# Query and key rows of the second attention kept so that a stack row is one 8 KB run in DRAM, read back whole in six transfers

## The reference

```python
Q, K, V = proj(wq, bq), proj(wk, bk), proj(wv, bv)     # [B, 16 heads, 512, 8]
scores = einsum('bhqd,bhkd->bhqk', Q, K) * scale
u = min(L, max(1, int(log(L))))                        # 6
top_u = top_k(scores.max(axis=-1), u)[1]               # the 6 queries with the largest score, per head
q_sel = take_along_axis(Q, top_u)
ctx = softmax(einsum('bhud,bhkd->bhuk', q_sel, K) * scale) @ V
out = zeros.at[top_u].set(ctx) @ wo.T + bo
```

## Time and profile before

| what | value |
|---|---|
| median of three runs | 1387.65 us (1384.28 to 1389.28) |
| the profiled execution: its own time | 1385.65 us |
| its span in the trace | 1383.8 us |
| granted TensorE clock, mean over the span | 0.871 |
| busy: PE, DVE, POOL, ACT | 81%, 75%, 64%, 55% |
| DMA: moved, mean rate | 176.65 MB, 128 GB/s |

### The profile page before, as it was taken

How to read it: one execution, slowest core, us unless ns; L and a number is a source line. 1 busy time by engine, 2 the same in 40 slices (tenths; PEclk the granted TensorE clock), 3 DMA queues, 4 the chain that set the end, 5 groups by cost and what they waited for, 6 DMA issues and landing times.

```text
span 1383.8 us, 27422 instructions
## 1 busy us (share of the span) xinstructions
PE 1121.0 (81%) x7574; PEld 696.9 (50%) x7574; DVE 1040.6 (75%) x4507; ACT 754.2 (55%) x1934; POOL 885.4 (64%) x1342
## 2 busy tenths in 40 slices
PE   3999999897999987888878888888888899999100
PEld 1555555564888972334333333334333379899100
DVE  2899999898475636899989999998988966565211
ACT  2444444342665655777766766766766657556000
POOL 3237776677553503567888888878785555367776
PEclk9999999999899995798898888977868789999655
DMA  6877621102465664444444444444444435577522
GB/s 177 220 192 192 164 70 60 51 31 57 121 187 176 191 174 120 118 112 102 114 105 107 107 112 114 115 120 114 105 105 97 132 89 162 160 217 213 150 76 78
DMA packets 176104, 176.65 MB, mean 128 GB/s; under 512 B 22736, under 2 KB 166224, under 8 KB 175952
## 3 DMA queue, kind: packets, MB, share of 16 engines
q1 hardware_dynamic: 159568, 141.19, 38.4%
q0 software_dynamic: 16384, 33.72, 8.8%
HBM read 83.91 MB, written 90.92 MB: 126 GB/s over the span
## 4 chain that ended last, share of the span: by engine, by line
PE 22%; DVE 21%; POOL 10%; ACT 6%; issue 5%; DMA 3%; SPq 2%; ACTq 0%; POOLq 0%; DVEq 0%
DVE pT L1544 13%; PE pair L2028 5%; PE pair L1951 5%; POOL tok L663 5%; POOL vmyg L663 5%; ACT pT L1059 3%; PE pair L1962 2%; PE pair L1940 1%; PE bank L2069 1%; PE bank L1752 1%; PE bank L2013 1%; DVE xs L1466 1%; SPq L461 1%; PE bank L1758 1%; PE bank L2034 1%
## 5 line engine op out<-in xcount | busy, mean ns | idle before, releaser
L1544 DVE CUSTOM_DVE_ANT_0 pT<-pair,pT 128x256 f32<-128x256 f32 x1024 | 379.6, 414 | 46.8 <-ACT pT L1059 44.3
L1059 ACT ACTIVATE pT<-pair 128x256 f32<-128x256 f32 x1024 | 322.9, 398 | 137.7 <-PE pair L2028 136.9
L1951 PE MATMUL pair<-xeT_sg,unit_w 128*128 128x256 f32 x768 | 183.4, 382 | 0.0
L1269 DVE TENSOR_TENSOR pT<-pair,causal 128x512 f32<-128x512 f32 x256 | 159.4, 679 | 15.5 <-PE pair L1813 15.2
L604 POOL DMA_INDIRECT dispA<-xnf,sli x128 | 128.4, 1003 | 53.9 <-issue 31.6
L2028 PE MATMUL pair<-whose,apart 64*128 64x512 bf16 x512 | 135.3, 454 | 33.7 <-DVE smax L1544 29.7
L604 POOL DMA_INDIRECT dispB<-xnf,sli x128 | 128.5, 1004 | 51.9 <-issue 30.7
L2028 PE MATMUL pair<-xeT_sg,apart 64*128 64x512 bf16 x512 | 132.9, 451 | 31.6 <-DVE smax L1544 30.8
L1436 DVE TENSOR_TENSOR hid<-xeT_sg,pair 128x512 f32<-128x512 f32 x96 | 65.9, 686 | 114.6 <-ACT xeT_sg L969 114.4
L1951 PEld LDWEIGHTS pair<-xeT_sg,unit_w 128*128 128x128 f32 x768 | 139.6, 192 | 15.2
L1962 PE MATMUL pair<-unit_w,hid 128*128 128x128 f32 x768 | 103.7, 279 | 12.1 <-DVE ye L1450 12.1
(11 more groups left out here) (257 smaller groups left out, 2382.9 us busy)
## 6 DMA issues: line engine op xcount, KB each, us to landing
dispB<-zeros SPq DMA_DIRECT2D x16, 1419.0 KB
apart<-dispA SPq DMA_DIRECT2D x96, 129.0 KB
apart<-dispB SPq DMA_DIRECT2D x96, 129.0 KB
ybufA<-ye SPq DMA_DIRECT2D x48, 256.0 KB
ybufB<-ye SPq DMA_DIRECT2D x48, 256.0 KB
apart<-q_rows SPq DMA_DIRECT2D x128, 96.0 KB
q_rows<-ctxT SPq DMA_DIRECT2D x64, 128.0 KB, 2.5
whose<-k_rows SPq DMA_DIRECT2D x64, 96.0 KB
```

The source lines that it names most:

```text
L1059: act.activation(rel[n % RING][:, q, :], pair[n % RING][:, q, HALF:SEQ], ACT.Relu).then_inc(s["relu_done"], 1)
L1269: dve.tensor_tensor(pT[n % (2 * NG)][:, :, :], bank[4 + n % 4].rearrange("p (j t) -> p j t", j=GH), causal[:, :].unsqueeze(1).to_broadcast ...
L1544: dve.tensor_tensor_reduce(out=rel[n % RING][:, q, :], in0=pair[n % RING][:, q, 0:HALF], in1=rel[n % RING][:, q, :], scale=1.0, scalar=LOW ...
L1951: last = pe.matmul(bank[3 + 2 * h + k][:, u * UR:(u + 1) * UR], unit_w[r][:, u, k * D:(k + 1) * D], xeT[h][:, UT * u:UT * (u + 1), :].rear ...
```

## The change

The DRAM tensors change from `[H, 5, DH, SEQ]` (head, slot, dimension, token) to `[5, P, SEQ]` (slot, row, token), and likewise for the keys. The rows of the projection come in a new order: the host permutes the columns of the turned weights `wq` and `wk` and the two biases, so that row = (head of a pair, dimension, pair) in place of (pair, head of a pair, dimension). The eight pairs of one dimension are now neighbours, and eight rows of 512 bf16 make one run of 8 KB, which is the whole of a stack row. A group is read for all eight blocks in one transfer, with the source seen as (slot, dimension, 4096 elements). A part that goes to two slots is written by one transfer with a broadcast source. That makes 3 + 3 writes and 6 + 6 reads a batch, 18 in place of 32. `scores` waits for both whole stacks at n = 0. In the first batch `keys_out(0)` comes before `queries_in(0)`, and `keys_in(0)` a group earlier. A second head mask `headofb` in the new order is made at the start. ACT loads the experts' numbers for group g + 3 after the copies of group g + 2, in place of those for g + 2 before them.

```diff
-Q_SLOTS = ((0, 3), (1, 4), (2,))
-K_SLOTS = ((0,), (1,), (2,))
+Q_SLOTS = (slice(0, 5, 3), slice(1, 5, 3), slice(2, 3))
+K_SLOTS = (slice(0, 1), slice(1, 2), slice(2, 3))
 Q_GROUPS = ((1, 3), (2, 3), (0, 2))
 K_GROUPS = ((0, 3), (0, 3), (0, 2))
-ROWS_IN = 16 * 2 * 2 * len(Q_GROUPS)
+ROWS_IN = 16 * 2 * len(Q_GROUPS)
...
-        q_rows = [nc.dram_tensor(f"q_rows{h}", [H, 5, DH, SEQ], BF16).ap() for h in range(2)]
+        q_rows = [nc.dram_tensor(f"q_rows{h}", [5, P, SEQ], BF16).ap() for h in range(2)]
...
-                    for slot in at:
-                        sp.dma_start(rows[n % 2][:, slot], part).then_inc(s[done], 16)
+                    to = rows[n % 2][at].rearrange("s p n -> p s n")
+                    sp.dma_start(to, part.unsqueeze(1).to_broadcast(list(to.shape))).then_inc(s[f"{kind}_rows_done"], 16)
...
-                t = slice(half * STACKS // 2, (half + 1) * STACKS // 2)
-                each = rows[n % 2].rearrange("(t g) s d n -> g (s d) t n", g=2)
+                sp.wait_ge(s[f"{kind}_rows_done"], ROWS_OUT * (n + 1))
                 for g in range(2):
                     at = g * NP * DH
                     for first, count in groups:
-                        sp.dma_start(stack[n % 2][at:at + count * DH, t, :], each[g][first * DH:(first + count) * DH, t, :]).then_inc(
-                            s[f"rows_in{2 * (n % 2) + half}"], 16)
+                        sp.dma_start(stack[n % 2][at:at + count * DH, :, :].rearrange("p t n -> p (t n)"),
+                                     rows[n % 2][first:first + count, g * P // 2:(g + 1) * P // 2, :].rearrange(
+                                         "s (d t) n -> s d (t n)", t=STACKS)).then_inc(s[f"{kind}_in{n % 2}"], 16)
...
                 if g == 18:
                     queries_out(0)
+                if g == 19:
+                    keys_out(0)
                 if g == 20:
                     queries_in(0)
-                    keys_out(0)
-                if g == 22:
+                if g == 21:
                     keys_in(0)
...
+            pool.memset(headposb[:, :, :, :], 0.0)
...
+            pool.affine_select(out=headposb[:, :, :, :], in_=headposb[:, :, :, :], compare_op=ALU.not_equal, fill=1.0, base=0,
+                               pattern=[[-1, H // 2], [-DH * (H // 2), 2], [-(H // 2), DH]], channel_multiplier=1)
...
                     if 2 <= g < G - 2:
-                        copies(g + 2, weights_of(mybir.EngineType.Activation, seg, g + 2, 1))
+                        copies(g + 2, ex)
+                    if 1 <= g < G - 3:
+                        ex = weights_of(mybir.EngineType.Activation, seg, g + 3, 1)
...
+            dve.tensor_reduce(headofb[:, :], headposb[:, :, :, :].rearrange("p t g d -> p (t g) d"), AX.X, ALU.add)
...
-                if n % (PAIRS // 2) == 0:
-                    pe.wait_ge(s[f"rows_in{2 * h + n // (PAIRS // 2)}"], ROWS_IN * (b // 2 + 1))
+                if n == 0:
+                    pe.wait_ge(s[f"q_in{h}"], ROWS_IN * (b // 2 + 1))
+                    pe.wait_ge(s[f"k_in{h}"], ROWS_IN * (b // 2 + 1))
...
+    for n in ("b_wqT", "b_wkT", "b_bq", "b_bk"):
+        rows = arrays[n].reshape(-1, H // 2, 2, DH).transpose(0, 2, 3, 1)
+        arrays[n] = np.ascontiguousarray(rows.reshape(arrays[n].shape))
```

More of the change, by code:

```diff
@@ L60 @@
 STACKS = H // 2
-Q_SLOTS = ((0, 3), (1, 4), (2,))
-K_SLOTS = ((0,), (1,), (2,))
+Q_SLOTS = (slice(0, 5, 3), slice(1, 5, 3), slice(2, 3))
+K_SLOTS = (slice(0, 1), slice(1, 2), slice(2, 3))
 Q_GROUPS = ((1, 3), (2, 3), (0, 2))
 K_GROUPS = ((0, 3), (0, 3), (0, 2))
-Q_OUT = 16 * 5
-K_OUT = 16 * 3
-ROWS_IN = 16 * 2 * 2 * len(Q_GROUPS)
+ROWS_OUT = 16 * 3
+ROWS_IN = 16 * 2 * len(Q_GROUPS)
 def build(nc, w, out):
@@ L88, in build @@
         ybuf = (ybufA, ybufB)
-        q_rows = [nc.dram_tensor(f"q_rows{h}", [H, 5, DH, SEQ], BF16).ap() for h in range(2)]
-        k_rows = [nc.dram_tensor(f"k_rows{h}", [H, 3, DH, SEQ], BF16).ap() for h in range(2)]
+        q_rows = [nc.dram_tensor(f"q_rows{h}", [5, P, SEQ], BF16).ap() for h in range(2)]
+        k_rows = [nc.dram_tensor(f"k_rows{h}", [3, P, SEQ], BF16).ap() for h in range(2)]
         xs = sb("xs", [P, NT, D])
@@ L124, in build @@
         headof = sb("headof", [P, H])
+        headposb = sb("headposb", [P, H // 2, 2, DH])
+        headofb = sb("headofb", [P, H])
         inturn = sb("inturn", [P, GH])
@@ L271, in build @@
                  "n_done q_done k_done kv_done einv_ready qT_ready turns_ready kT_ready lefts past_done unit_w_act tok_ready vm_ready pv_done sc_done pT_ready state_done stm_ready ctxT_ready o_done "
-                 "bproj_done b_consts q_first q_left q_second q_third k_first k_left k_second k_third q_rows_done k_rows_done rows_in0 rows_in1 rows_in2 rows_in3 bkT_ready selrow_done xsel_done att_scaled ffn_scaled xselq_ready xctx_done xctx_ready bsc_done relu_done bmax_done vbias_done vout_done voutb_done mT_done mTs_done m8_done m8i_done m8f_done idg_done "
+                 "bproj_done b_consts q_first q_left q_second q_third k_first k_left k_second k_third q_rows_done k_rows_done q_in0 q_in1 k_in0 k_in1 bkT_ready selrow_done xsel_done att_scaled ffn_scaled xselq_ready xctx_done xctx_ready bsc_done relu_done bmax_done vbias_done vout_done voutb_done mT_done mTs_done m8_done m8i_done m8f_done idg_done "
                  "idx_done idc_done sel_done qsel_done qsel_ready att_done amax_done aneg_done aexp_done aeT_done aeT_ready cx_done cx_ready "
@@ L441, in begin, with rows_out, rows_in @@
                     load(seg, r)
-            def rows_out(n, rows, parts, slots, ready, done):
+            def rows_out(n, kind, rows, parts, slots):
                 if n >= 2:
[L447 to L450, removed]
-                    for slot in at:
-                        sp.dma_start(rows[n % 2][:, slot], part).then_inc(s[done], 16)
-            def rows_in(n, rows, stack, groups, half):
-                t = slice(half * STACKS // 2, (half + 1) * STACKS // 2)
-                each = rows[n % 2].rearrange("(t g) s d n -> g (s d) t n", g=2)
+                    sp.wait_ge(s[f"{kind}_in{n % 2}"], ROWS_IN * (n // 2))
+                for part, at, nth in zip(parts, slots, ("first", "second", "third")):
+                    sp.wait_ge(s[f"{kind}_{nth}"], n + 1)
+                    to = rows[n % 2][at].rearrange("s p n -> p s n")
+                    sp.dma_start(to, part.unsqueeze(1).to_broadcast(list(to.shape))).then_inc(s[f"{kind}_rows_done"], 16)
+            def rows_in(n, kind, rows, stack, groups):
+                sp.wait_ge(s[f"{kind}_rows_done"], ROWS_OUT * (n + 1))
                 for g in range(2):
@@ L460, in rows_in @@
                     for first, count in groups:
-                        sp.dma_start(stack[n % 2][at:at + count * DH, t, :], each[g][first * DH:(first + count) * DH, t, :]).then_inc(
-                            s[f"rows_in{2 * (n % 2) + half}"], 16)
+                        sp.dma_start(stack[n % 2][at:at + count * DH, :, :].rearrange("p t n -> p (t n)"),
+                                     rows[n % 2][first:first + count, g * P // 2:(g + 1) * P // 2, :].rearrange(
+                                         "s (d t) n -> s d (t n)", t=STACKS)).then_inc(s[f"{kind}_in{n % 2}"], 16)
                         at += count * DH
             def queries_out(n):
-                rows_out(n, q_rows, q_part, Q_SLOTS, ("q_first", "q_second", "q_third"), "q_rows_done")
+                rows_out(n, "q", q_rows, q_part, Q_SLOTS)
             def keys_out(n):
-                rows_out(n, k_rows, k_part, K_SLOTS, ("k_first", "k_second", "k_third"), "k_rows_done")
+                rows_out(n, "k", k_rows, k_part, K_SLOTS)
             def queries_in(n):
-                sp.wait_ge(s["q_rows_done"], Q_OUT * (n + 1))
                 if n >= 2:
                     sp.wait_ge(s["bsc_done"], 2 * PAIRS * (n - 1))
-                for half in range(2):
-                    rows_in(n, q_rows, qst, Q_GROUPS, half)
+                rows_in(n, "q", q_rows, qst, Q_GROUPS)
             def keys_in(n):
-                sp.wait_ge(s["k_rows_done"], K_OUT * (n + 1))
-                for half in range(2):
-                    rows_in(n, k_rows, kst, K_GROUPS, half)
+                rows_in(n, "k", k_rows, kst, K_GROUPS)
             def first_stack(g):
@@ L767, in queries_third @@
                 if n:
-                    pool.wait_ge(s["q_rows_done"], Q_OUT * n)
+                    pool.wait_ge(s["q_rows_done"], ROWS_OUT * n)
                 pool.tensor_tensor(q_part[2], q_rest[:, :], q_part[1], ALU.subtract).then_inc(s["q_third"], 1)
@@ L778, in keys_third @@
                 if n:
-                    pool.wait_ge(s["k_rows_done"], K_OUT * n)
+                    pool.wait_ge(s["k_rows_done"], ROWS_OUT * n)
                 pool.tensor_tensor(k_part[2], k_rest[:, :], k_part[1], ALU.subtract).then_inc(s["k_third"], 1)
@@ L1006, in queries @@
                     act.wait_ge(s["q_left"], n)
```

(6 more changed lines are left out.)

## The result

| | before | after |
|---|---|---|
| median | 1387.33 us (1384.28 to 1389.28, 4 runs) | 1730.21 us (1729.23 to 1734.04, 4 runs) |
| profiled execution, span | 1385.65, 1383.8 us | 1730.87, 1729.1 us |
| first scores of batch 0 | 525.24 | 543.21 |
| mean distance of two batches | 37.12 us | 58.94 us |
| from batch 15's first scores to the end | 301.75 us | 301.81 us |

The change makes the kernel slower: 1.2479 times the time before, 95% interval 1.2449 to 1.2509. The prediction was 1805 us, with 1705 to 1975 as its range.

What follows compares the result with a forecast made beforehand. The prediction took DVE, not transfers, to bound attention B before the change; the profiled 1385.65 + 395 for attention B's batches + 23 at the handoff gave 1804, stated as 1805 us, range 1705 to 1975.

Steps and rivals of the forecast that it cites:

- The mechanism: Stack reads in attention B use 3 and 2 DMA engines, not 12 and 16, making batches 63.4 us apart: +395 us.
- Rival (1): Stack reads: engines chosen by the 24 partitions alone, 12 and 16 as now; attention B stays DVE's; 1376 us, chance 0.10.
- rival (2): Stack reads: the eight dimensions are dealt, giving 8 engines and 39.2 us a batch; 1412 us, chance 0.03.
- first scores to queries' reads: Attention B batch: time until the queries' reads are issued, set by DVE, PE and POOL, which stay; 19.9 us.
- queries' reads to keys' reads: Attention B batch: queries' reads 18.2 us, keys' writes waiting behind them 1.0, plus start, landing and scatters; 22.2 us.
- keys' reads to next scores: Attention B batch: keys' reads 18.2 us, plus start, landing and scatters, before the next batch's scores; 21.3 us.
- the time of a run: One 8 KB run on one DMA engine in a stack's reads: 0.38 us, bounded by 0.34 and 0.49.
- the one lone packet: The single 8 KB packet that a trace view isolates: 0.42 us, used in choosing a run's time.
- The bound from the full rate: All engines full move 386 GB/s, 24.1 GB/s each, so an 8 KB run takes 0.34 us; forecast then 1743.
- The handoff: Experts to attention B: stores stand behind the first stacks' reads; first scores at 548.3 rather than 525.24, +23 us.
- The rest: Whole-stack wait, broadcast writes, SP's reads, ACT's loads and the start's mask add 0, ACT's within 3 us.
- rival (3): Engines as now, but second halves come late for n = 0, beginning where a stack's reads exceed 7.7 us; 1386, chance 0.02.

Runs made afterwards that it cites:

- the three experiments with other shapes: Changed kernel with the head outermost in DRAM (1429.96 us), with one read per slot (1613.22 us), and with each stack as two 64-row reads (1409.65 us).
- The first experiment: Changed kernel with the head of a pair outermost in DRAM for queries and keys, so slot and dimension merge, each part written per head: 1429.96 us.
- the second experiment: The kernel of the first experiment with its reads cut into 1 KB packets in place of 8 KB: 1450.39 us.
- the 128-row kernel: Changed kernel with parts written to DRAM for all eight pairs, so a whole stack is one read of 128 rows: 1385.58 us, 0.9998 of the kernel before.

## Why the prediction was right

**The mechanism: right, step by step.** The divisor of the outermost sizes of both sides gave 3 and 2 engines, and 16 end marks a stack; 16 were counted. The same rule gave 80, 128 and 32 in the three experiments with other shapes, all as counted. It is the rule of the Trainium skill, DMA: Bandwidth & Descriptors, section "Why a DMA increments its semaphore by 16 and not by 1", and the traces agree, now down to two engines. Rival (1), engines by the 24 partitions alone, fell with the first count. So did rival (2), eight engines.

**The batch's terms.**

| term of the batch | predicted | measured, mean of 15 |
|---|---|---|
| first scores to queries' reads | 19.9 | 18.9 (16.5 to 21.6) |
| queries' reads to keys' reads | 22.2 | 20.5 (18.8 to 21.0) |
| keys' reads to next scores | 21.3 | 19.6 (18.7 to 20.5) |
| sum | 63.4 | 58.9 |

The predicted second and third lines are 18.2 for 48 runs, 2.1 for start and landing, half of the scatters' 1.9, and in the second the keys' writes, 1.0. The mis-sized term is the time of a run: I took 0.38, between the full rate and the one lone packet, and it is 0.345. 48 x 0.035 = 1.7 us a stack is the whole error of either line. The bound from the full rate, 386 GB/s over 16 engines, was the right one: three engines alone move as much each, 8192 B in 0.345 us or 23.7 GB/s, as 16 do at their best, 24.1. The lone packet of 0.42 us belonged to another queue and misled me. The other error is 1.0 us in the compute before the reads, inside the 17.6 to 20.7 that batches before had shown. Together 4.5 us in each of 15 batches, 67 of the 75 us by which 1805 was too long.

**The handoff: right in its steps, 18.0 for 23.** Queries' reads issued at 504.32 rather than 506.0 give 1.7 back, and two stacks of 48 runs 3.4; with these the written sum comes to 543.2, the time measured. That it fits so closely is luck, since two errors of about 1 us cancel: the store behind the stacks landed at 539.46 where the corrected sum has 540.6, and between the last two results DVE waited 2.23 us where I had 1.2 for PE's product.

**The rest at nothing: right.** After the last batch the two kernels take the same to 0.1 us, and ACT's numbers alone made no difference. SP's six reads took 4.24 us and not 2.4; the batch's sum comes out without them, as written.

**Where the reasoning was wrong, without showing in the number.** Rival (1) priced 12 and 16 engines at 5 us a stack and came to 1376 us. The first experiment has these engines, and takes 9.1 us from the keys' first issue to the scores and 1430 us. The earlier trace rows could have told me: 0.630 x 16 x 7.6 / 128 is 0.60 us for 8 KB, beside the 0.34 of the earlier trace rows. I read these lines for the count and not for the price, took "engines not full" for spare time, and so believed that more engines are always faster. Rival (2) took over the same price, 0.38 us a run on eight engines, and came to 1412 us; eight engines took 0.80 a run, and 1613. The prediction also saw nothing to gain from the longer run, and the second experiment, where many engines write to few partitions, shows 20 us for it. And rival (3) was put at a point, "begins where a stack's reads take over 7.7 us", that I thought out of reach: with 12 or 16 engines it is reached. The first experiment's reads of the keys are issued 30.4 us into a batch, the 128-row kernel's 30.0; 9.1 more is past the 37.1 that DVE sets and 5.2 more is not. That is why the one loses 2.46 us in every batch, and the other nothing. Two readings were loose, and nothing hangs on them: the prediction sets five writes of the first stacks between the stores, the queries' alone, where there are eight; and of the fifteen later first scores in the kernel before, the trace names DVE's maximum before nine, not nearly all; at five PE shows no idle time.

What a run of 8 KB takes, by the shape of the read, from the windows above:

| rows of a read | engines | us a run | keys' first issue to next scores, mean | kernel |
|---|---|---|---|---|
| 24 and 16, by three and two slots (after) | 3 and 2 | 0.345 | 19.6 | 1730 |
| 8 | 8 | 0.80 | 16.0 | 1613 |
| 24 and 16 | 12 and 16 | 0.67 | 9.1 | 1430 |
| 64 | 16 | 0.62 | 7.6 | 1410 |
| 128 | 16 | 0.38 | 7.1, of which 5.2 to landing | 1386 |

The windows hold one stack each; over all fifteen keys' reads of a trace the means are, in the table's order, 0.36, 0.79, 0.65, 0.59 and 0.40 us. The last line of the table is no longer set by the reads; in the others the scores start 0.1 us after the reads' last landing in nearly every batch.

## What to carry to other kernels

Before a transfer gets longer runs, count how many engines it will use from the outermost size of both its sides, and check the count in a window of the trace by its end marks: here the same bytes in an eighth of the packets cost 25%, because three slots became the outermost size of the source. Then price a run in that window as share x engines x time over runs: many engines on few partitions took 0.6 to 0.8 us where 0.35 to 0.38 was possible, so a transfer wants both many engines and all 128 partitions. A mean DMA share that falls while the time rises is the sign that a few engines do all the work.

## What the runs showed of the hardware that I had not expected

- A run took longer where many engines wrote into few partitions. For 8 KB it was 0.345 us with three engines on 24 partitions, 0.67 with 12, 0.80 with eight on eight partitions, and 0.62 with 16 on 64 partitions; 16 on 128 took 0.38. That the engines share ports is argued from the shapes and not seen port by port.
- On few partitions long runs help: 1 KB packets in place of 8 KB, on the same engines and partitions, cost 1450.39 against 1429.96 us.
- The issue of a read on SP isn't a constant. For the six reads of the kernel after, its median was 0.68 us; for the same rows with slot and dimension merged 0.36, and for the kernel before 0.375.
